# A Mamba scan that keeps its states in SBUF, with a six-tile ring and half of the C products shared between two engines

## The reference, cut to what matters

```python
dt = softplus(dt @ dt_w + dt_b);  A = -exp(A_log)
dA  = exp(dt[..., None] * A)                              # (b, t, 512, 16)
dBu = dt[..., None] * B_ssm[:, :, None, :] * xc[..., None]
h = dAt * h + dBut                                        # over t
y = einsum('bdn,bn->bd', h, ct)                           # sum over the 16 states
return y + xc * D_skip
```

## Time and profile before

| what | us |
|---|---|
| median of three executions | 3791.1 |
| the profiled execution, as timed | 3796.9 |
| its span, first to last instruction | 3795.1 |
| DVE busy | 3057.4 (81%) |
| PE busy | 2855.8 (75%) |
| ACT busy | 1991.5 (52%) |
| POOL busy | 1949.1 (51%) |

### The profile page before, as it was taken

How to read it: one execution, slowest core, us unless ns; L and a number is a source line. 1 busy time by engine, 2 the same in 40 slices (tenths; PEclk the granted TensorE clock), 3 DMA queues, 4 the chain that set the end, 5 groups by cost and what they waited for, 6 DMA issues and landing times.

```text
span 3795.1 us, 41535 instructions
## 1 busy us (share of the span) xinstructions
PE 2855.8 (75%) x12965; PEld 1467.3 (39%) x12965; DVE 3057.4 (81%) x4262; ACT 1991.5 (52%) x3811; POOL 1949.1 (51%) x1115
## 2 busy tenths in 40 slices
PE   7963877689776987679776897769866797765436
PEld 3631444245423553245442454235532454422103
DVE  5354889797988989788897979888897888979765
ACT  2533665446653575546654466535755466544332
POOL 2014754556545654447545565456544475456671
PEclk9976988899987998799988999879987999887657
DMA  3007885966668665867759666786658677597890
GB/s 94 1 17 209 212 221 159 273 159 179 175 205 240 174 179 152 252 166 193 206 150 272 160 177 175 204 240 175 180 153 247 168 192 208 144 269 209 233 246 19
DMA packets 373277, 691.40 MB, mean 182 GB/s; under 512 B 52157, under 2 KB 63552, under 8 KB 366912
## 3 DMA queue, kind: packets, MB, share of 16 engines
q1 hardware_dynamic: 373056, 688.74, 67.3%
HBM read 603.65 MB, written 84.93 MB: 181 GB/s over the span
## 4 chain that ended last, share of the span: by engine, by line
PE 42%; DVE 27%; ACT 9%; issue 7%; POOL 7%; DMA 6%; SPq 1%; POOLq 0%; ACTq 0%; DVEq 0%
PE banks L1387 22%; DVE banks L943 7%; PE banks L1579 5%; PE banks L1392 5%; POOL sb_arena L1074 4%; DVE sb_arena L950 4%; PE banks L1657 4%; PE banks L1555 3%; ACT banks L1355 3%; ACT sb_arena L1121 2%; DMA sb_arena<-kept_u 2%; PE banks L1427 2%; DVE sb_arena L652 2%; PE banks L1401 2%; DVE sb_arena L847 2%
## 5 line engine op out<-in xcount | busy, mean ns | idle before, releaser
L1074 POOL TENSOR_TENSOR sb_arena<-sb_arena 128x1024 f32<-128x1024 f32 x512 | 1205.6, 2359 | 970.3 <-PE banks L1657 605.5
L943 DVE TENSOR_TENSOR_SCAN banks<-banks,sb_arena 128x512 f32<-128x512 f32 x999 | 1171.4, 1217 | 277.0 <-ACT banks L1355 203.5
L1355 ACT ACTIVATE banks<-sb_arena,sb_neg_a 128x512 f32<-128x512 f32 x1024 | 665.1, 682 | 982.8 <-DVE sb_arena L950 792.0
L1657 PE MATMUL banks<-sb_arena,sb_w_sum 128*32 128x512 f32 x2048 | 336.5, 729 | 461.7 <-DVE sb_arena L950 363.4
L950 DVE TENSOR_TENSOR sb_arena<-banks,sb_arena 128x512 f32<-128x512 f32 x999 | 636.8, 678 | 0.0
L1392 PE MATMUL banks<-sb_ident,sb_arena 128*128 128x128 f32 (+1 forms) x2083 | 358.5, 296 | 364.3 <-POOL sb_arena L984 153.2
L1121 ACT ACTIVATE sb_arena<-banks 128x512 f32<-128x512 f32 (+2 forms) x720 | 360.6, 517 | 510.7 <-PE banks L1392 344.8
L1392 PEld LDWEIGHTS banks<-sb_ident,sb_arena 128*128 128x128 f32 (+1 forms) x2083 | 242.4, 148 | 575.0 <-ACT sb_arena L1121 224.4
L801 DVE TENSOR_REDUCE sb_nmax<-banks 128x1 f32<-128x512 f32 (+3 forms) x352 | 222.7, 635 | 187.0 <-PE banks L1582 186.5
L1387 PE MATMUL banks<-sb_w_gu,sb_arena 128*128 128x352 f32 x1024 | 362.5, 505 | 5.5 <-ACT sb_arena L1121 5.5
L1579 PE MATMUL banks<-sb_arena 128*128 128x384 f32 (+3 forms) x1024 | 361.1, 464 | 4.5 <-POOL sb_arena L1001 4.5
(11 more groups left out here) (132 smaller groups left out, 4020.9 us busy)
## 6 DMA issues: line engine op xcount, KB each, us to landing
sb_arena<-kept_dt SPq DMA_DIRECT2D x1024, 256.0 KB, 5.2
sb_arena<-kept_u SPq DMA_DIRECT2D x1024, 256.0 KB, 4.6
kept_xc<-sb_arena SPq DMA_DIRECT2D x16, 1024.0 KB, 4.9
kept_z<-sb_arena SPq DMA_DIRECT2D x16, 1024.0 KB, 5.5
sb_arena<-kept_xc SPq DMA_DIRECT2D x64, 256.0 KB, 5.6
kept_dt<-sb_arena SPq DMA_DIRECT2D x64, 256.0 KB, 3.9
kept_u<-sb_arena SPq DMA_DIRECT2D x64, 256.0 KB, 3.9
sb_arena<-kept_z SPq DMA_DIRECT2D x63, 256.0 KB, 5.8
```

The source lines that it names most:

```text
L943: v.tensor_tensor_scan(products if e == 1 and shared(K) else factors, factors, products, 0.0, ALU.mult, ALU.add).then_inc(V.sem, V.mark("s ...
L1074: nc.gpsimd.tensor_tensor(dBu[K % SLOTS], rows_u[K % US], bt[:, gd % 2].unsqueeze(1).to_broadcast([P, 2, T]), ALU.mult).then_inc(G.sem, G. ...
L1355: nc.scalar.activation(psum[:, e], rows_dt[K % RS][:, e], ACT.Exp, scale=neg_a[:, s, m, j:j + 1]).then_inc(A.sem, A.mark("dA", K, e))
L1657: mm = pe.matmul(psum[r:r + L, YB], w_sum[:, L * o:L * o + L], dBu[k % SLOTS][:, e], start=(o == 0), stop=(o == QG - 1))
```

## The change

- **Scan into SBUF.** Both halves are now scanned out of PSUM factors and the SBUF u*B tile *into that same tile*. The factors in PSUM are free again when the scan is done, so `factors(K + 1, e)` waits for `scan(K, e)` and no longer for the product.
- **One ring of six.** The u rows are loaded into the ring tile itself, POOL multiplies by B in place, DVE scans in place, the C product is in place, and PE sums it. `SLOTS` = 6 takes the place of 4 product tiles and 2 row tiles, with the same SBUF bytes. The load of u for K now waits for `summed(K - 6)`; `make_dBu` waits for the load alone.
- **The product, one scan later.** `weigh(K - 1)` stands behind `scan(K, 0)` and is one 128x1024 instruction with both inputs in SBUF. For every odd unit of every sequence (`SHARED` from 1 on) DVE multiplies only the first half (128x512) and POOL the second (`weigh_state`).
- **Side steps between the halves.** DVE's first group of side steps of a unit now stands between `scan(K, 0)` and `scan(K, 1)`. ACT makes the two halves of the factors with side steps in between. POOL's `weigh_state` stands behind the first side steps, not ahead of them.
- **4 KB rows.** dt and u are stored in DRAM so that the two halves of a unit lie side by side. A spread is then one DMA of 512 KB with rows of 4 KB in place of two of 256 KB; a store is four DMAs in place of one.
- **The table.** `VISITS` holds other numbers, with the same sums (183, 230 and 65 steps).

```diff
-SLOTS, US, RS = 4, 2, 3
+SLOTS, RS = 6, 3
-SHARED = tuple(range(15, NU, 2))
+SHARED = tuple(range(1, NU, 2))
...
-    "middle": "0012003103011116093755733052020212123201040107405110222120313130"
+    "middle": "1020200201300012051433950213632720041012003301210133211122210124"
...
         def shared(K):
-            return K >= NK - NU and K % NU in SHARED
+            return K % NU in SHARED
...
             def store_dt(g):
                 sp.wait_ge(G.sem, G.at("dt", g))
-                sp.dma_start(kept_dt[g], dt).then_inc(s_kept_dt, 16)
+                for r in range(QG):
+                    sp.dma_start(blocks_of(kept_dt[g], r), dt[L * r:L * r + L]).then_inc(s_kept_dt, 16)
...
             def spread_u(K):
                 g, q = divmod(K, NQ)
                 if q == 0:
-                    sp.wait_ge(s_kept_u, 16 * (g + 1))
-                if K >= US:
-                    sp.wait_ge(G.sem, G.at("dBu", K - US))
-                for e in range(2):
-                    sp.dma_start(rows_u[K % US][:, e], over_states(kept_u[g], q, e)).then_inc(s_u[K % US], 16)
+                    sp.wait_ge(s_kept_u, 16 * QG * (g + 1))
+                if K >= SLOTS:
+                    sp.wait_ge(E.sem, summed(K - SLOTS))
+                sp.dma_start(tiles[K % SLOTS].rearrange("p e t -> p (e t)"), over_states(kept_u[g], q)
+                             ).then_inc(s_u[K % SLOTS], 16)
...
                     if K + RS < NK:
                         spread_dt(K + RS)
-                    if K + US + 2 < NK:
-                        spread_u(K + US + 2)
+                    if K >= 2 and K % 2 == 0:
+                        for n in (K - 2 + SLOTS, K - 1 + SLOTS):
+                            if n < NK:
+                                spread_u(n)
...
+            def scan(K, e):
+                factors, states = psum[:, e], tiles[K % SLOTS][:, e]
+                if K // (DT * NQ) % 2 == 1:
+                    factors, states = factors[:, ::-1], states[:, ::-1]
+                if e == 0:
+                    v.wait_ge(G.sem, G.at("dBu", K))
+                v.wait_ge(A.sem, A.at("dA", K, e))
+                v.tensor_tensor_scan(states, factors, states, 0.0, ALU.mult, ALU.add
+                                     ).then_inc(V.sem, V.mark("scan", K, e))
+
+            def weigh(K):
+                gd = K // (DT * NQ)
+                n = 1 if shared(K) else 2
+                if K % (DT * NQ) == 0:
+                    v.wait_ge(s_ct[gd % 2], 16 * (gd // 2 + 1))
+                v.wait_ge(V.sem, V.at("scan", K, n - 1))
+                v.tensor_tensor(tiles[K % SLOTS][:, 0:n], tiles[K % SLOTS][:, 0:n],
+                                ct[:, gd % 2].unsqueeze(1).to_broadcast([P, n, T]), ALU.mult
+                                ).then_inc(V.sem, V.mark("hc", K))
...
+                    scan(K, 0)
+                    if K >= 1:
+                        weigh(K - 1)
                     advance(side, visits[2 * k])
-                    for e in range(1 if shared(K) else 2):
-                        if e == 0 and K % (DT * NQ) == 0:
-                            v.wait_ge(s_ct[gd % 2], 16 * (gd // 2 + 1))
-                        v.wait_ge(V.sem, V.at("scan", K, e))
-                        v.tensor_tensor(dBu[K % SLOTS][:, e], psum[:, e], ct[:, gd % 2], ALU.mult
-                                        ).then_inc(V.sem, V.mark("hc", K, e))
+                    scan(K, 1)
...
             def make_dBu(K):
                 gd = K // (DT * NQ)
-                g.wait_ge(s_u[K % US], 32 * (K // US + 1))
-                if K >= SLOTS:
-                    g.wait_ge(E.sem, summed(K - SLOTS))
+                g.wait_ge(s_u[K % SLOTS], 16 * (K // SLOTS + 1))
...
                     if K + 2 < NK:
                         make_dBu(K + 2)
+                    advance(side, visits[2 * k])
                     if shared(K):
                         weigh_state(K)
-                    advance(side, visits[2 * k])
...
-                if K >= 1 and e == 1 and shared(K - 1):
+                if K >= 1:
                     a.wait_ge(V.sem, V.at("scan", K - 1, e))
-                elif K >= 1:
-                    a.wait_ge(V.sem, V.at("hc", K - 1, e))
...
                     if K + 1 < NK:
                         factors(K + 1, 0)
-                        factors(K + 1, 1)
...
                     advance(side, visits[2 * k + 1])
+                    if K + 1 < NK:
+                        factors(K + 1, 1)
...
-                pe.wait_ge(V.sem, V.at("hc", K + 1, 0 if shared(K + 1) else 1))
+                pe.wait_ge(V.sem, V.at("hc", K + 1))
```

More of the change, by code:

```diff
@@ L263, in hybrid_block @@
         xcr = area(2, T)
-        rows_u, rows_dt = [area(2, T) for _ in range(US)], [area(2, T) for _ in range(RS)]
+        rows_dt = [area(2, T) for _ in range(RS)]
         bt, ct = area(2, T), area(2, T)
-        dBu = [area(2, T) for _ in range(SLOTS)]
+        tiles = [area(2, T) for _ in range(SLOTS)]
         at_xT = place[0]
@@ L323, in hybrid_block @@
         s_kept_dt, s_kept_u = sem("dt_stored"), sem("u_stored")
-        s_u = [sem(f"u_spread_{i}") for i in range(US)]
+        s_u = [sem(f"u_spread_{i}") for i in range(SLOTS)]
         s_dt = [sem(f"dt_spread_{i}") for i in range(RS)]
@@ L553, in store_dt, with blocks_of, over_states @@
                 sp.wait_ge(G.sem, G.at("dt", g))
-                sp.dma_start(kept_dt[g], dt).then_inc(s_kept_dt, 16)
+                for r in range(QG):
+                    sp.dma_start(blocks_of(kept_dt[g], r), dt[L * r:L * r + L]).then_inc(s_kept_dt, 16)
             def store_u(g):
                 sp.wait_ge(G.sem, G.at("u", g))
-                sp.dma_start(kept_u[g], u).then_inc(s_kept_u, 16)
-            def over_states(kept, q, e):
-                r = CT * row_block(q, e)
-                return kept[r:r + CT].unsqueeze(0).to_broadcast([DS, CT, T])
+                for r in range(QG):
+                    sp.dma_start(blocks_of(kept_u[g], r), u[L * r:L * r + L]).then_inc(s_kept_u, 16)
+            def blocks_of(kept, r):
+                return kept[r // 2::2, :, r % 2]
+            def over_states(kept, q):
+                return kept[q].rearrange("c e t -> c (e t)").unsqueeze(0).to_broadcast([DS, CT, 2 * T])
             def spread_u(K):
@@ L576, in spread_dt @@
                 if q == 0:
-                    sp.wait_ge(s_kept_dt, 16 * (g + 1))
+                    sp.wait_ge(s_kept_dt, 16 * QG * (g + 1))
                 if K >= RS:
                     sp.wait_ge(A.sem, A.at("dA", K - RS, 1))
-                for e in range(2):
-                    sp.dma_start(rows_dt[K % RS][:, e], over_states(kept_dt[g], q, e)).then_inc(s_dt[K % RS], 16)
+                sp.dma_start(rows_dt[K % RS].rearrange("p e t -> p (e t)"), over_states(kept_dt[g], q)
+                             ).then_inc(s_dt[K % RS], 16)
             def load_states(gd):
@@ L590, in load_states @@
                 if gd >= 2:
-                    sp.wait_ge(V.sem, V.at("hc", last_of(gd - 2), 1))
+                    sp.wait_ge(V.sem, V.at("hc", last_of(gd - 2)))
+                    if shared(last_of(gd - 2)):
+                        sp.wait_ge(G.sem, G.at("hc", last_of(gd - 2)))
                 sp.dma_start(ct[:, gd % 2], rows_bc[b, s, DS:2 * DS].unsqueeze(1).to_broadcast([DS, CT, T])
@@ L601, in _ @@
             store_u(0)
-            for K in range(US):
+            for K in range(2):
                 spread_u(K)
             load_z(1)
-            for K in range(US, US + 2):
+            for K in range(2, SLOTS):
                 spread_u(K)
@@ L933, in _ @@
                     g, q = divmod(K, NQ)
-                    gd = g // DT
-                    back = gd % 2 == 1
-                    for e in range(2):
-                        factors, products = psum[:, e], dBu[K % SLOTS][:, e]
-                        if back:
-                            factors, products = factors[:, ::-1], products[:, ::-1]
-                        if e == 0:
-                            v.wait_ge(G.sem, G.at("dBu", K))
-                        v.wait_ge(A.sem, A.at("dA", K, e))
-                        v.tensor_tensor_scan(products if e == 1 and shared(K) else factors, factors, products, 0.0,
-                                             ALU.mult, ALU.add).then_inc(V.sem, V.mark("scan", K, e))
-                    advance(side, visits[2 * k])
-                    for e in range(1 if shared(K) else 2):
-                        if e == 0 and K % (DT * NQ) == 0:
-                            v.wait_ge(s_ct[gd % 2], 16 * (gd // 2 + 1))
-                        v.wait_ge(V.sem, V.at("scan", K, e))
-                        v.tensor_tensor(dBu[K % SLOTS][:, e], psum[:, e], ct[:, gd % 2], ALU.mult
-                                        ).then_inc(V.sem, V.mark("hc", K, e))
+                    scan(K, 0)
+                    if K >= 1:
+                        weigh(K - 1)
+                    advance(side, visits[2 * k])
+                    scan(K, 1)
```

(1 more changed line is left out.)

25 lines of the change are left out of this document (13 added, 12 removed).

## The result

The changed kernel took 4078.95 us (median of 4; 4075.07 to 4087.89), the kernel before 3790.89 us beside it: 288 us slower, ratio 1.076, 95% interval 1.0737 to 1.0784. The forecast was 3722 us, in a range of 3560 to 3860. The measured time lies 219 us above that range and also above the slowest rival (3886 us); "slower" had a chance of 0.30.

What follows compares the result with a forecast made beforehand. DVE was taken as first limit in most of a sequence, PE in a fifth. 3796.9 - 168 - 20 + 246 - 108 - 19 = 3728, less 5.8 to the median, gave 3722 us, range 3560 to 3860.

Steps and rivals of the forecast that it cites:

- the slowest rival: DVE's two-SBUF products each meeting POOL at the shared port, full price 410 us: 3886 us, chance 0.17.
- The bound: DVE is the first limit in most of a sequence, PE in a fifth; DVE busy 377.8 of 441.7 us.
- Item 1: C products on DVE, fewer and larger out of SBUF: 469 us in place of 637, 168 us saved.
- Item 2: Scans on DVE writing into SBUF: 1197 ns against 1217, 20 us saved.
- Item 3: Port shared by DVE and POOL: 512 two-SBUF products, 0.60 of them waiting 0.80 us, 246 us lost.
- Item 4: Decay factors freed by the scan: two thirds of DVE's 203.5 us of waits go, 108 us saved after a deduction.
- item 6: DMA with 4 KB rows and half the spreads: worth at most 23 us, put at 0.
- Item 5: Tail of the last sequence, units 28 to 62: six tiles untie u*B from PE's sum, 19 us saved.
- Nothing is left: Rival: DVE's gain turns up as waits for scores, PE and POOL; 3791 us, chance 0.05.
- the port did decide: Rival: at 0.61 us a product, DVE's port waits with POOL eat the 315 us of gains; chance 0.17.
- PE's sum did wait longer: Rival: PE's state sum waits for a later DVE product and for POOL's, 122 us; 3844 us, chance 0.11.

Runs made afterwards that it cites:

- run 13: Changed kernel with 2 KB rows, DVE's products reading PSUM bank 0 in place of C, first factors waiting for an earlier product: 3778.9 us, ratio 0.997.
- run 14: Kernel before with the ring of six, 2 KB rows, and POOL's product for every odd unit of all sequences: 3818.3 us, ratio 1.008.
- run 11: Changed kernel with the rows of before, two spreads of 256 KB in 2 KB rows and one store DMA: 4012.1 us.
- run 1: Kernel before with both scans writing to SBUF, the 128x512 products reading two SBUF inputs, and the next factors waiting for the scan: 4144.8 us.
- run 12: Kernel before with the ring of six alone, u*B in place, 2 KB rows, scans and products over PSUM: 3789.1 us, ratio 0.9995.
- run 10: Changed kernel with the second half of the factors made right behind the first on ACT: 4218.6 us.
- run 7: Kernel before with the 4 KB rows alone: one spread of 512 KB for two of 256 KB, four store DMAs for one: 3910.5 us, ratio 1.032.
- run 9: Kernel before with the new DRAM layout and its four store DMAs, spreads still two of 256 KB in 2 KB rows: 3846.2 us, ratio 1.014.
- run 3: Changed kernel with the VISITS table of before: 4325.1 us.
- run 4: Kernel before with the VISITS table of the changed kernel: 4105.8 us.
- run 2: Kernel before with POOL making the second half's product in every odd unit of all sequences, ring of four kept: 3923.9 us.

## Why the prediction was wrong

**The bound (right, and then not heeded).** DVE sets the time in most of a sequence, but with 64 us of idle in 442 and with PE, ACT and POOL all tied to it unit by unit. Taking work off DVE moved the time little in runs 13 and 14: 133 us less DVE work gave 12 us, 125 us less gave a loss.

**Item 1, products on DVE (size right).** The undisturbed products of run 13 are 1194 and 660 ns and 475 us in all; the estimate was 1224 and 691, less 41 ns of overlap that did not come, and 469 us.

**Item 2, scans (failed, small).** The mean is 1211 ns for 1217, where the item took the 1197 of 25 scans. The busy time is 1231 us for 1201 of all scans before, since they no longer stand back to back and overlap. Not 20 us saved but 30 lost.

**Item 3, the port (mechanism right, size too small on DVE).** The sum had 0.48 us a product and 246 us. The changed kernel has 767 - 475 = 292 us over the products of run 13: 0.57 us a product, 0.45 for those of 1024 and 0.69 for those of 512. How often a product waits was right: 319 of the 512 took over 0.1 us more than the shortest of their size, 0.62 for 0.60. How long was too short: 0.92 us for 0.80 on average. Run 13 against run 11 puts the port at 233 us of time, inside the bounds of 0 and 410. That this lies near the 246 is partly luck: there DVE had 332 us less, 0.65 us a product, and not all of it became time. This was not what failed. Where the rule of the Trainium skill ("SBUF — State Buffer", "Who interferes with whom") has the second instruction blocked until the first has finished, the trace agrees in kind; it can also be blocked longer (last section).

**Item 4, the factors (failed in sign).** "Two thirds of 203.5 go" held in run 1, where the order stayed: 76 us were left. The changed kernel has 273 us. Of these, 114 go with the 2 KB rows (run 11: 160 us), so over half of this failure belongs to item 6; 160 is still well above the 68 that item 4 would leave. The mean of 0.9 us was read wrongly as well: some 190 of the 236 waits of before are under a microsecond, but they hold only 76 us, and 20 waits of over 2 us hold 92. Why the new order leaves 160 us is open. The second half of the factors stands behind a whole set of side steps because `scan(K, 1)` does, and the dt row is given back only then. SP waited 956 us for ACT to free a dt row, before 308. But in run 12 SP waited 625 us for that at no cost in time, and in run 10, with the second half made early, 569 us in a slower kernel. In the changed kernel SP also waited 530 us for PE's sum ahead of u rows, with dt rows behind them in its queue; no run took that away in the new order.

**Item 5, the tail (right by itself, failed in the changed kernel).** The stretch of the last sequence from its first to its last scan was 332 us before, 367 after, 335 in run 13. The ring alone (run 12) took 327, and from unit 28 to unit 62 it took 155.4 us for 162.5: 7 us saved, in the range of 5 to 37. The 4 KB rows alone (run 7) made them 180 us, as they are in the changed kernel.

**Item 6, the rows (failed in sign).** I bounded them by 0 and 23 us of gain and named as the danger only that cover might go. With their stores they cost 67 us in the changed kernel and 118 in the kernel before, there about half of it by the layout and its stores. One DMA of 512 KB for two of 256 KB means that nothing is there until nearly 8 us after the issue, in place of some 6. Four small stores stand in front of the first spread of a group: SP waited 93 us for stored u rows in run 9, before 71. In a kernel that takes 4.8 us a unit in its last sequence, with three dt rows and the next spread issued only when one is free, 2 us of landing can reach DVE; that they do is read from the waits of run 7, where ACT's for dt rows and DVE's for factors both grow. The item asked only what DVE's wait for u*B could gain, and not what a later landing of dt would do to ACT's 190 us of waits and, through them, to DVE's 203.

**The sum.** Run 11, run 13 and the kernel before make a chain of three differences: 67 us for the rows, 233 for the port in the kernel with 2 KB rows, and -12 for all else. That they add up to 288 is so by construction and proves nothing; in another order the shares may be others, as 67 against 118 for the rows shows. The prediction had 0, +246 and -315 us for the same three, items 1, 2, 4 and 5 being the last. So 303 of the 357 us by which it missed lie in that last term. Its failed step is to have counted DVE time as time of the kernel, and the waits that go as waits that stay gone. Run 13 shows what came in place: DVE was 133 us less busy than before, it was 108 us more idle, its wait for factors was 273 us and not 68 (some of it by this run's own delay of the first factors), and the time fell by 12. The prediction had named this ("Nothing is left", its fourth rival) and gave it 0.05, though with a port price that the gain covers; here the port came on top. Of its other rivals, the port did decide. In the changed kernel its price was below the 0.61 us a product at which it was said to, because nothing was left on the other side. And PE's sum did wait longer, 658 us for DVE, with 463 us of its weight loads waiting for POOL; what that cost in time no run separates.

**What stays open.** Run 13 delays the first factors by up to a product (ACT waits 280 us for it), so the order may be worth more than 12 us; by how much is not shown. No table was fitted to any variant; 246 and 313 us in runs 3 and 4 say that fitting one could move runs 2, 13 and 14 by more than the differences that are told here. Why the split by stores and spreads is 55 to 64 was not taken further. The mean granted clock of PE is lower in the slower runs (0.829 in run 3, 0.841 in run 1, 0.871 before, 0.878 in run 13), and what slower matmuls add is inside every figure here; no run separates it.

## What to carry to other kernels

When a product moves from PSUM to SBUF to save a few nanoseconds, count where both of its operands lie: with two in SBUF it and GpSimd's instructions held each other up, 1250 ns for 678 on average. Before you credit an engine's saved time, undo the cost side by an experiment and look at whether the time follows; here, where the engines step through a fixed order together, it went to waits. And a larger DMA is only better if throughput is what is missing: here the later landing was paid at once.

## What the runs showed that I had not expected

**One instruction can be passed over several times.** A 128x512 product (0.66 us undisturbed) of the changed kernel in the timeline (start us, us, instruction):

```profile
1872.62 1.29 POOL L1096 TENSOR_TENSOR sb_arena<-sb_arena 128x512 f32<-128x512 f32 x1
1872.86 1.21 DVE L887 TENSOR_TENSOR_SCAN sb_arena<-banks,sb_arena 128x512 f32<-128x512 f32 x1
...
1873.85 1.31 POOL L1017 TENSOR_TENSOR sb_arena<-sb_arena 128x512 f32<-128x512 f32 x1
...
1873.99 8.16 DVE L896 TENSOR_TENSOR sb_arena<-sb_arena 128x512 f32<-128x512 f32 x1
...
1875.09 4.66 POOL L1089 TENSOR_TENSOR sb_arena<-sb_arena 128x1024 f32<-128x1024 f32 x2
1879.69 1.91 POOL L1031 TENSOR_TENSOR sb_arena<-sb_arena,sb_own_rows 128x1024 f32<-128x1024 f32 x1
1882.07 1.21 DVE L887 TENSOR_TENSOR_SCAN sb_arena<-banks,sb_arena 128x512 f32<-128x512 f32 x1
```

The product starts at 1873.99, 0.14 us after L1017, and ends at 1882.15, 0.55 us after the last of four POOL instructions that ran back to back. I had reckoned with the rest of one instruction. The longest of the 512 products:

```profile
L896 DVE TENSOR_TENSOR sb_arena<-sb_arena x512: 658/1200/8176, 336.9 to 4003.3; 128x1024 f32<-128x1024 f32 x86, 128x512 f32<-128x512 f32 x85
```

This is the exception. It comes four times in the trace at the same place of the order, and a fifth product took 6.3 us in the same way, each time behind an L1017 that had started 0.10 to 0.32 us earlier; the five hold 36 of the 292 us. Twice the same meeting took 1.73 us. As a rule DVE does get in between, though POOL has the next instruction ready: in the earlier trace rows L1055 and L1060 follow each other within 0.1 us, L652 has its turn, and L1060 is the one that is stretched. Why the five are passed over is not shown.

**Longer rows were not cheaper.** Run 7 moved the same bytes in fewer packets, and the queue's share of the DMA engines' time over the span was no smaller for it: 67.3% of 3795 us before, 2554 us, and 69.1% of 3906 us there, 2699 us. The two lines are from the page of before and of run 7:

```profile
q1 hardware_dynamic: 373056, 688.74, 67.3%
```

```profile
q1 hardware_dynamic: 225600, 688.68, 69.1%
```
